# One constant matmul of 384 columns behind each of the 69 hops of a walk back

## The chip, the cores and the metric

The kernel runs on one core of a Trainium2 chip. The metric is the device time of one execution in microseconds (us); the figure of a kernel is the median of its runs.

## The reference, cut to what matters

Two gated layers over a hidden state of 8 batches of 56 tokens of 128 numbers, with a context of 8 x 1500 rows of 128 numbers. The first step aligns the 1500 context rows of a batch with its 56 tokens by dynamic time warping: a cost matrix, a path walked back from its last cell, and the context rows summed per token along the path.

```python
D = _pairwise_euclidean(small, large)
R = _dtw_cost(D)              # R[i,j] = D[i,j] + min(up, left, diagonal)
i_idx, j_idx, valid = _backtrack(R, T_small, T_large)
contrib = small[i_idx] * valid[:, None]
expanded = zeros((T_large, d)).at[j_idx].add(contrib)
...
x = x + tanh(g_xattn[0]) * _L0_xattn_ref(ctx_1024, layernorm(x))   # the alignment
x = x + tanh(g_ffn[0]) * _L0_ffn_ref(layernorm(x), ...)            # memory of 8192 rows, best row per head
x = x + tanh(g_xattn[1]) * _L1_xattn_ref(layernorm(x), ctx, ctx)   # attention, 16 heads, needs keys and values of ctx
x = x + tanh(g_ffn[1]) * _L1_ffn_ref(layernorm(x), ...)            # 8 experts
```

## The kernel before, in words

The program is written out by hand, one block per engine, with semaphores between them; there is no planner, so the order of the source is the order of each queue.

The alignment puts 16 lanes of a batch on 16 partitions (8 batches, 128 partitions), a lane holding C = 100 context rows. VectorE (DVE) scans the cost matrix in STEPS = 70 steps, step by step. TensorE (PE) meanwhile projects the keys of the attention layer (`keys_of`, `take_off`) and turns comparisons into jump codes (`jump_codes`, L1343 to L1347: three float16 matmuls with 404 or 400 columns, the first of `one16` by `steps16`, both constants). The codes go into banks 2 and 3; DVE reads each (`jump_targets`) and so gets, for every row, where the path leaves the lane.

Then the walk back: 69 hops, h = 0 to 68. Per hop DVE finds the entry for each lane (L1214, a comparison over 202 numbers with an accumulated sum, which reads the result of the last hop as its scalar from bank 2) and raises `s_hit`; PE spreads it over the lanes of the batch by one float16 matmul of one column with the constant weights `blk16` (L1403), and raises `s_hop`, for which the next L1214 waits. In between, PE works off the value projections (L1356, float32, 128 rows of context by the 128 columns of `Wv_sb`): there are 96 of them, 16 come before the walk and 80 in it. So 58 hops are followed by one value and 11 by two. A value shows as two records in the trace. ScalarE (ACT) copies groups of four out of their banks (L679). In the queue of PE the part around the change reads:

```python
pe.wait_ge(s_hit, h + 1)
nc.tensor.matmul(ps[2][:, t - 1:t], blk16[:, :], acc[:, t - 1:t], ...).then_inc(s_hop, 1)
...
for i in range(values, due):
    value(i)
```

After the walk DVE places the results (L1220, L1223), PE spreads them in two float32 matmuls of 284 columns (L1415, into banks 0 and 1), DVE copies them (L1229), and PE folds two weight matrices into bank 3 (L1421, eight float32 matmuls of 64 columns). ACT (L691) and DVE (L1238) then make 60 masks, 15 for each of four groups, and PE sums context rows under them (L1434), group by group; the masks of a third group wait until the sums of the first are done. Then come the layer norm (L1253, L1259), the memory layer with its gathers on GpSimd (POOL, L543), attention and the experts.

Bank 3 is read for the last time before the walk by the last `jump_targets` on DVE, which stands ahead of the first L1214 in DVE's queue; it is written next by the fold L1421.

Of the kernel before, what the change touches and what calls it, by code (L numbers as in the profile page):

```python
# [27 lines left out]
def build_gated_layers(nc, x_T, ctx_T, ctx_nat, g_xattn, g_ffn, weights, fold_w, w_tab, W1, W2, out):  # L28
# [5 lines left out]
    C = 100  # L34
# [18 lines left out]
    TB = 5  # L53
# [45 lines left out]
    with ExitStack() as ctx:  # L99
        def sb(name, shape, dt=F32):  # L100
            return ctx.enter_context(nc.sbuf_tensor(name, shape, dt))
# [5 lines left out]
        ps = [banks[:, i, :] for i in range(8)]  # L107
# [52 lines left out]
        steps16 = sb("steps16", [P, TB * SLOT], F16)  # L160
# [14 lines left out]
        def weight(n):  # L175
            nonlocal at
            at += n
            return wts[:, at - n:at]

        Wk_sb, cols = weight(D), weight(3)  # L180
# [14 lines left out]
        one16 = sb("one16", [P, P], F16)  # L195
# [229 lines left out]
        def _(sp):  # L425
# [23 lines left out]
            def load_key_parts(b):  # L449
                for c, (kx, _) in enumerate(PRODUCTS):  # L450
                    if b < 2 and c >= 2:
                        sp.wait_ge(s_kpl[b][c % 2], 16 * (c // 2))
                    sp.dma_start(KP[b % 3][c:NPR:len(PRODUCTS), :, :],
                                 key_parts[b, kx].rearrange("(m r) i -> r m i", r=2 * DH)
                                 ).then_inc(s_kpl[b % 3][c % 2], 16)
# [355 lines left out]
        def _(ve):  # L811
# [88 lines left out]
            def memory_layer():  # L900
# [42 lines left out]
                for c, (_, qx) in enumerate(PRODUCTS):  # L943
                    last = nc.vector.tensor_copy(picks[:, :, qx, c::len(PRODUCTS)], own)
# [305 lines left out]
        def _(pe):  # L1250
# [29 lines left out]
            def turn(u):  # L1280
# [6 lines left out]
                                               sd[:, u % D_RING, s * C:(s + 1) * C], ident[:, :])  # L1287
                last.then_inc(s_turn, 1)

            pe.wait_ge(s_mw, 1)  # L1290
            pe.wait_ge(s_x, 16)
            for i, (lo, hi) in enumerate(PAIR_COLS):
# [57 lines left out]
            def value(i):  # L1350
                n, k = i // 4, i % 4
                b, c = i // NCH, i % NCH
                if k == 0 and n >= 6:
                    pe.wait_ge(s_vc, n - 5)
                rows = min(P, NI - c * P)
                last = nc.tensor.matmul(ps[VALUE_BANKS[n % 6]][0:rows, k * D:(k + 1) * D],  # L1356
                                        ctxT[:, b * NI + c * P:b * NI + c * P + rows], Wv_sb, start=True, stop=True)
                if k == 3:
                    last.then_inc(s_vp, 1)
# [40 lines left out]
            for h in range(STEPS - 1):  # L1400
                t = STEPS - 1 - h
                pe.wait_ge(s_hit, h + 1)
                nc.tensor.matmul(ps[2][:, t - 1:t], blk16[:, :], acc[:, t - 1:t], start=True, stop=True  # L1403
                                 ).then_inc(s_hop, 1)
                if h == 0:
                    pe.wait_ge(s_kx[2], NKP)
                due = EARLY_VALUES + (h + 1) * (NB * NCH - EARLY_VALUES) // (STEPS - 1)
                for i in range(values, due):
                    value(i)
                values = due  # L1410
# [3 lines left out]
            for half in range(2):  # L1414
                last = nc.tensor.matmul(ps[half][0:C, 0:NB // 2 * ZW], ones[:, 0:C],  # L1415
                                        zt[:, half * NB // 2:(half + 1) * NB // 2, :].rearrange("p b j -> p (b j)"),
                                        start=True, stop=True)
# [147 lines left out]
            for b in range(NB):  # L1565
                pe.wait_ge(s_nmc, b + 1)
                for c in range(NCH):
# [5 lines left out]
                    for m in range(NH // 2):  # L1573
                        if m % 4 == 0 and len(units) > 1:
                            row_scores(*units.pop(0))
                        bank = ps[2 + 2 * (g % 2) + m // (NH // 4)]
# [135 lines left out]
```

## Time and profile before

| | before |
|---|---|
| median of 3 runs | 553.11 us (550.53, 553.89, 553.11) |
| the profiled execution | 552.93 us |
| its span, first to last instruction | 551.2 us |
| mean granted clock of TensorE over the span | 0.849 |
| PE busy | 425.8 us (77%), 3768 matmul records |
| DVE busy | 375.4 us (68%) |
| ACT busy | 262.9 us (48%) |
| POOL busy | 86.1 us (16%) |

All times in rows count from the first instruction of the profiled execution. A record of a matmul runs from its start to a modelled end, and matmuls are pipelined, so records overlap and a row merges those that touch. A granted clock of 1.00 is 2.4 GHz, 0.50 is 1.2 GHz. "Idle before" in brackets is the time that an engine stood still, with what released it.

### The profile page before, as it was taken

The page shows a single profiled execution, that of the slowest core. Times are in us where ns is not written, and L with a number is a line of the kernel's source. Part 1 is how long each engine was busy: PE and PEld are TensorE (multiplying, and loading weights), DVE is VectorE, ACT ScalarE, POOL GpSimd, SP SyncE. Part 2 cuts the span into 40 slices and gives each one's busy share as a digit, 9 for nine tenths or more (in the row PEclk, how much of TensorE's full clock was granted, in tenths as well). Part 3 has the DMA queues.
Part 4 walks back from the last instruction along what each step waited for, and adds up shares of the span by engine and source line. Part 5 has one row for each costly group of instructions (what it writes and reads, how often), then busy time and mean ns, then how long its engine had stood idle before and what let it go on. Part 6 is the DMA issues. An engine that isn't in the chain of part 4 may idle for free.

```text
span 551.2 us, 9665 instructions
## 1 busy us (share of the span) xinstructions
PE 425.8 (77%) x3768; PEld 253.9 (46%) x3768; DVE 375.4 (68%) x993; ACT 262.9 (48%) x449; POOL 86.1 (16%) x101
## 2 busy tenths in 40 slices
PE   3997887658999796300328789989999999779995
PEld 1443333326777594100113356656666666444442
DVE  7557999997555684876676668878889882361112
ACT  4365888665322491100101166656666667524442
POOL 2000000001000005687970000210210211000000
PEclk9999999998555687655558599999999999959999
DMA  8500564325412104953170002572573490000000
GB/s 288 202 1 1 172 202 156 107 84 153 135 57 68 44 3 111 220 149 88 35 168 0 0 1 39 133 167 56 119 168 83 90 298 11 3 0 0 0 1 17
DMA packets 28701, 50.03 MB, mean 91 GB/s; under 512 B 2448, under 2 KB 18384, under 8 KB 28656
## 3 DMA queue, kind: packets, MB, share of 16 engines
q1 hardware_dynamic: 26832, 45.74, 31.1%
q0 software_dynamic: 1536, 3.67, 2.5%
q8 instruction: 30, 0.49, 0.4%
q14 instruction: 15, 0.12, 0.1%
q10 hardware_dynamic: 288, 0.00, 0.0%
HBM read 39.96 MB, written 9.45 MB: 90 GB/s over the span
## 4 chain that ended last, share of the span: by engine, by line
PE 53%; DVE 30%; issue 7%; POOL 6%; ACT 2%; DMA 1%; DVEq 0%; POOLq 0%
PE banks L1356 9%; PE banks L1526 7%; PE banks L1550 7%; DVE mx L1005 6%; POOL arena L543 6%; PE banks L1578 5%; DVE arena L1185 5%; PE banks L1620 5%; PE banks L1628 4%; PE banks L1494 3%; PE banks L1271 2%; DVE work L1180 2%; PE banks L1434 2%; PE banks L1275 2%; DVE arena L1181 2%
## 5 line engine op out<-in xcount | busy, mean ns | idle before, releaser
L1005 DVE TENSOR_REDUCE mx<-banks 112x1 f32<-112x500 f32 x192 | 121.2, 675 | 25.4 <-PE banks L1526 25.4
L769 ACT ACTIVATE arena<-banks 128x896 f32<-128x896 f32 x96 | 87.9, 917 | 49.2 <-PE banks L1578 48.5
L1526 PE MATMUL banks<-ctxT,arena 128*112 128x500 bf16 x144 | 57.6, 411 | 7.4 <-issue 3.4
L1356 PE MATMUL banks<-wts,ctxT 128*128 128x128 f32 x192 | 57.9, 442 | 0.0
L1550 PE MATMUL banks<-arena 128*32 128x112 f32 (+1 forms) x1536 | 57.1, 265 | 1.0 <-ACT arena L769 0.8
L1214 DVE SCALAR_TENSOR_TENSOR work<-twice,banks,arena 128x202 f32<-128x202 f32 x68 | 29.5, 434 | 22.7 <-PE banks L1403 22.7
L1356 PEld LDWEIGHTS banks<-wts,ctxT 128*128 128x128 f32 x192 | 44.2, 295 | 1.0 <-ACT arena L679 0.3
L1550 PEld LDWEIGHTS banks<-arena 128*32 128x32 f32 (+1 forms) x1536 | 33.6, 109 | 21.1 <-issue 18.4
L1578 PEld LDWEIGHTS banks<-arena,ctxT 128*128 128x128 bf16 (+1 forms) x576 | 37.4, 104 | 10.5 <-issue 2.8
L1578 PE MATMUL banks<-arena,ctxT 128*128 128x112 bf16 (+1 forms) x576 | 40.9, 213 | 0.6 <-issue 0.6
L543 POOL DMA_INDIRECT arena<-in_w_tab,idx x32 | 33.9, 1060 | 12.6 <-issue 9.4
L1185 DVE TENSOR_TENSOR_SCAN arena<-work,arena 128x100 f32<-128x100 f32 x70 | 29.8, 426 | 7.4 <-ACT work L622 5.0
L1326 PE MATMUL banks<-arena,minusb 128*128 128x375 bf16 x64 | 19.9, 331 | 17.8 <-ACT arena L631 15.0
L637 ACT ACTIVATE arena<-banks,wts 128x375 bf16<-128x375 f32 x64 | 33.4, 581 | 0.5 <-PE banks L1326 0.5
L784 ACT ACTIVATE arena<-banks,wts 128x448 f32<-128x448 f32 x32 | 20.2, 633 | 27.2 <-PE banks L1620 27.2
L679 ACT ACTIVATE arena<-banks 128x512 f32<-128x512 f32 (+2 forms) x32 | 14.2, 493 | 38.1 <-PE banks L1356 35.7
L1620 PE MATMUL banks<-xnT,arena 128*128 128x448 f32 x64 | 32.2, 593 | 0.0
L1480 PE MATMUL banks<-ident,x_tok 112*128 112x112 f32 x4 | 1.2, 414 | 38.1 <-DVE x_tok L961 38.1
L1526 PEld LDWEIGHTS banks<-ctxT,arena 128*112 128x112 bf16 x144 | 18.7, 130 | 24.6 <-issue 11.9
L1628 PE MATMUL banks<-arena 128*128 128x448 f32 x64 | 29.6, 548 | 0.0
L1136 DVE SCALAR_TENSOR_TENSOR xc<-banks,wts,arena 128x448 f32<-128x448 f32 x7 | 4.8, 684 | 35.3 <-PE banks L1628 35.3
L576 POOL TENSOR_TENSOR work<-arena,mk 128x448 f32<-128x448 f32 x7 | 6.5, 932 | 133.1 <-ACT arena L746 133.1
(253 smaller groups left out, 741.3 us busy)
## 6 DMA issues: line engine op xcount, KB each, us to landing
ctxT<-key_parts SPq DMA_DIRECT2D x36, 375.0 KB, 6.5
key_parts<-arena SPq DMA_DIRECT2D x32, 281.2 KB, 2.8
ctxT<-in_ctx_T SPq DMA_DIRECT2D x12, 500.0 KB, 8.8
arena<-key_parts SPq DMA_DIRECT2D x12, 375.0 KB, 7.3
ctxT<-in_ctx_nat SPq DMA_DIRECT2D x5, 750.0 KB
arena<-in_ctx_nat SPq DMA_DIRECT2D x3, 750.0 KB
arena<-in_L_ffn_W SPq DMA_DIRECT2D x1, 2048.0 KB, 9.5
arena<-in_fold_w SPq DMA_DIRECT2D x1, 768.0 KB, 6.0
```

The source lines that it names most:

```text
L543: nc.gpsimd.indirect_dma_start(out=gath[:, t, h, :], out_offset=None, in_=w_tab[:, :], in_offset=bass.IndirectOffsetOnAxis(ap=idx[:, c:c + ...
L637: nc.scalar.activation(kq[m % STORES][:, x, :], ps[KBANKS[m % KRING]][:, 0:KPIECE], ACT.Identity, bias=cols[:, 1:2]).then_inc(s_kx[x], 1)
L769: nc.scalar.activation(Pt[0:rows, g % 2, :].rearrange("p (a n) -> p a n", a=2), banks[0:rows, 2 + 2 * (g % 2):4 + 2 * (g % 2), 0:HQ // 2], ...
L1005: nc.vector.tensor_reduce(mx3[:, b % 2, u // NPIECE, u % NPIECE:u % NPIECE + 1], ps[k % (6 if b == 0 else 2)][0:2 * NJ, 0:PIECE], AX_X, AL ...
L1185: nc.vector.tensor_tensor_scan(view(R, [[1, C]], (t + 1) * SLOT + 1), m, d, R[:, (t + 1) * SLOT:(t + 1) * SLOT + 1], ALU.min, ALU.add).the ...
L1214: nc.vector.scalar_tensor_tensor(out=hit_at.rearrange("p (c k) -> p c k", k=2), in0=twice[:, :].rearrange("p (c k) -> p c k", k=2), scalar ...
L1356: last = nc.tensor.matmul(ps[VALUE_BANKS[n % 6]][0:rows, k * D:(k + 1) * D], ctxT[:, b * NI + c * P:b * NI + c * P + rows], Wv_sb, start=T ...
L1526: nc.tensor.matmul(ps[k % ring][0:2 * NJ, 0:PIECE], QP[:, u // NPIECE, b, :], KP[b % 3][:, u // NPIECE, (u % NPIECE) * PIECE:(u % NPIECE + ...
L1550: last = nc.tensor.matmul(ps[6 + b % 2][q:q + 32, o:o + 2 * NJ], vals[0:rows, v0:v0 + 32], Pt[0:rows, g % 2, 2 * t * NJ:2 * (t + 1) * NJ], ...
L1578: last = nc.tensor.matmul(bank[0:rows, o:o + 2 * NJ], KP[b % 3][:, m, c * P:c * P + rows], QP[:, m, b, :], start=True, stop=True)
L1620: nc.tensor.matmul(ps[5 + i % 2][:, 0:TOK], W1s[:, e, c * P:(c + 1) * P], xnT[:, :], start=True, stop=True).then_inc(s_h, 1)
L1628: nc.tensor.matmul(ps[7 if e % 2 else 0][:, 0:TOK], W2s[:, i, :], hT[:, i % 4, :], start=(c == 0), stop=(c == FC - 1)).then_inc(s_yu, 1)
```

## The change

Behind each hop's matmul PE issues one more: `one16` (128 x 128, float16) as weights, the first 384 columns of `steps16` (float16) as the moving operand, into bank 3, with no semaphore wait and none raised. Nobody reads what it writes. It stands ahead of the values of that hop; there are 69 of them.

```diff
+            def keep_busy(bank, n, cols=TB * C):
+
+                for _ in range(n):
+                    nc.tensor.matmul(bank[:, 0:cols], one16[:, :], steps16[:, 0:cols], start=True, stop=True,
+                                     skip_group_check=True)
+
...
                 pe.wait_ge(s_hit, h + 1)
                 nc.tensor.matmul(ps[2][:, t - 1:t], blk16[:, :], acc[:, t - 1:t], start=True, stop=True
                                  ).then_inc(s_hop, 1)
+                keep_busy(ps[3], 1, 384)
                 if h == 0:
                     pe.wait_ge(s_kx[2], NKP)
```

## Rows read from the trace of the kernel before

**Rows 1.** The page: tenths of PE busy, and granted clock, in 40 slices.
```profile
PE   3997887658999796300328789989999999779995
...
PEclk9999999998555687655558599999999999959999
```

**Rows 2.** Stretches: busy us of PE, PEld, DVE, ACT, POOL; clock; DMA share; GB/s.
```profile
100.00:120.00 20.00, 12.87 (x55) 5.97 (x53) 19.26 (x76) 13.28 (x27) 0.00 (x0) 1.00 0.29 96
...
130.90:132.50 1.60, 1.14 (x8) 0.77 (x9) 0.89 (x4) 1.57 (x3) 0.00 (x0) 1.00 0.97 257
132.50:183.80 51.30, 51.30 (x218) 39.04 (x217) 29.33 (x132) 14.48 (x32) 1.59 (x3) 0.50 0.36 105
183.80:187.20 3.40, 3.40 (x13) 2.48 (x12) 1.31 (x4) 0.65 (x2) 0.00 (x0) 0.51 0.00 0
187.20:192.70 5.50, 1.72 (x16) 1.58 (x15) 4.97 (x17) 4.66 (x16) 0.00 (x0) 0.80 0.00 1
192.70:198.50 5.80, 5.70 (x64) 5.74 (x66) 4.24 (x15) 5.80 (x22) 0.00 (x0) 0.60 0.01 3
198.50:211.00 12.50, 11.63 (x186) 10.16 (x182) 8.12 (x31) 9.03 (x33) 0.00 (x0) 1.00 0.01 2
```

**Rows 3.** The chain that ended last, in the walk: start, us, what.
```profile
133.27 0.64 PE banks L1356 x2
```

**Rows 4.** Groups by line, 130.9 to 183.9 us: busy, mean ns, idle before.
```profile
L1214 DVE SCALAR_TENSOR_TENSOR work<-twice,banks,arena 128x202 f32<-128x202 f32 x68 | 29.5, 434 | 22.7 <-PE banks L1403 22.7
...
L1403 PE MATMUL banks<-acc,blk 128*128 128x1 f16 x69 | 13.1, 190 | 1.1 <-DVE work L1214 1.1
```

**Rows 5.** Instructions in order of time, two hops at the half clock.
```profile
150.16 0.10 PEld L1403 LDWEIGHTS banks<-acc,blk 128*128 128x128 f16 x1 [0.20 <-DVE work L1214]
150.16 0.19 PE L1403 MATMUL banks<-acc,blk 128*128 128x1 f16 x1
...
150.21 1.20 PE L1356 MATMUL banks<-wts,ctxT 128*128 128x128 f32 x4
...
150.38 0.43 DVE L1214 SCALAR_TENSOR_TENSOR work<-twice,banks,arena 128x202 f32<-128x202 f32 x1 [0.28 <-PE banks L1403]
150.74 0.09 DVE L1214 DVE_READ_ACCUMULATOR work<-twice,banks,arena 128x1 f16 x1
...
151.20 0.21 PE L1403 MATMUL banks<-acc,blk 128*128 128x1 f16 x1
...
151.28 0.78 PE L1356 MATMUL banks<-wts,ctxT 128*128 128x128 f32 x2
...
151.95 0.10 PEld L1403 LDWEIGHTS banks<-acc,blk 128*128 128x128 f16 x1 [0.20 <-DVE work L1214]
```

**Rows 6.** Matmuls in order of time, at the full clock.
```profile
127.74 0.34 PE L1343 MATMUL banks<-steps,one 128*128 128x404 f16 x1 [0.57 <-DVE work L1163]
127.92 0.33 PE L1345 MATMUL banks<-work,one 128*128 128x400 f16 x1
...
130.94 0.18 PE L1403 MATMUL banks<-acc,blk 128*128 128x1 f16 x1 [0.72 <-DVE work L1214]
130.98 0.47 PE L1356 MATMUL banks<-wts,ctxT 128*128 128x128 f32 x2
131.66 0.18 PE L1403 MATMUL banks<-acc,blk 128*128 128x1 f16 x1 [0.21 <-DVE work L1214]
```

**Rows 7.** Instructions in order of time, from the last hop to the masks.
```profile
183.84 0.19 PE L1403 MATMUL banks<-acc,blk 128*128 128x1 f16 x1
...
184.93 2.22 PE L1415 MATMUL banks<-work,ones 128*100 128x284 f32 x4
...
187.19 0.81 DVE L1229 COPY work<-banks 100x284 f32<-100x284 f32 x2 [1.78 <-PE banks L1415]
```

**Rows 8.** Instructions in order of time, where the sums begin.
```profile
192.80 5.78 PE L1434 MATMUL banks<-arena 100*56 100x128 f32 x61 [3.88 <-issue]
...
198.53 7.55 DVE L1238 SCALAR_TENSOR_TENSOR arena<-work,rowc 100x112 f32<-100x112 f32 x30 [1.18 <-PE banks L1434]
```

## The prediction

> **What bounds the kernel now.** I read the page's slices first [rows 1]: PE is busy in nine tenths of the slices of the walk, and yet its clock stands at 0.5 there. The stretches say it more closely [rows 2]: 1.00 in the keys stage and in the first 1.6 us of the walk, then 0.50 in the whole of 132.5 to 183.8 us, where the records of PE cover 51.30 us of 51.30. That cover is not load: the records of matmuls reach beyond the array's own work.
>
> The chain of waits puts most of a hop on the value matmuls [rows 3], which would make PE the bound. The instructions in order of time correct this [rows 5]. In the usual hop PE's weight load for the hop has stood idle for 0.20 us and is released by DVE (row of 151.95): the loop is DVE's 0.43 us, the 0.09 us of the accumulator read and the hop's own 0.19 us with the hand-overs between. The groups agree: 68 comparisons take 29.5 us and wait another 22.7 us for the hop [rows 4]. So the walk is a loop of latencies between DVE and PE, and values ride along in its gaps.
>
> Two things in this loop depend on PE's clock. First, a hop with two values. At the half clock one value's records end 0.78 us after their start and two values' 1.20 us [rows 5]: 0.42 to 0.43 us per value. After two of them the next hop comes 151.20 - 150.16 = 1.04 us after the last, where a usual gap is 0.725 us, and it is not released by DVE but stands behind the values. Second, a little in each gap: at the full clock it is 131.66 - 130.94 = 0.72 [rows 6], more closely 0.717 us in the first three gaps, against 0.725 to 0.727 at the half clock. The gap behind a late hop is itself 0.03 us longer.
>
> **The change, part by part.** It removes and moves nothing. It adds 69 matmuls of 384 float16 columns with one weight load each, no wait and no semaphore. DVE, ACT, POOL and SP issue the same instructions in the same order.
>
> *(a) Cost of one.* Two matmuls of 404 and 400 columns start 127.92 - 127.74 = 0.18 us apart at the full clock [rows 6], so 384 columns take about 0.17 us there, and 0.33 us at half. Its weight load has no row of its own kind; I bound it between nothing (hidden, as the value matmuls at 0.43 us apart leave no sign of theirs) and 0.10 us, the hop's own weight load [rows 5]. I take 0.03.
>
> *(b) Does it lie on the loop?* It stands behind the hop, so it can only delay the next one. After the hop, the array's work apart from values is 1.04 - 2 x 0.427 = 0.19 us. At the full clock, one value: 0.19 + 0.21 + 0.17 + 0.03 = 0.60 us, under 0.717: hidden behind DVE's comparison. Two values: 0.81 us, 0.09 over. But the 0.19 was read at the half clock and part of it (the 0.10 us weight load) should shrink; the other reading, by the end of the records (0.05 + 0.47 + 0.21 + 0.17 less the 0.2 us by which a hop starts ahead of the end of the values), gives 0.70, no delay. I take 0.04 us for each of ten such gaps (the eleventh double hop is the last): **+0.4 us**, bounds 0 and +1.1.
>
> *(c) What it does to the clock.* This is the point of decision. In the first 1.6 us of the walk the engine was still at 1.00 from the keys stage and fell after two hops with values alone; the array then had 0.25 us of value work in 0.717 (80 values over 69 hops, 0.213 us each). With the filler it has 0.25 + 0.17 = 0.42 us, 58% of the hop. The keys stage holds 1.00 with records that cover 12.87 of 20 us [rows 2], which overstate the array's part just as they do here, so the filled walk is at least as loaded as a stage that never fell. And should the clock fall nevertheless before the walk, the filled hop at half clock is nearly all work (0.495 + 0.33 of about 0.94 us), like 183.8 to 187.2, where values, the spread and the fold followed one another and the clock rose at the end [rows 2]. I forecast 1.00 through the walk.
>
> By the Trainium skill (TensorE: Matmul & The Clock Gate, Why this matters for your kernels) drops come from long pauses between bursts of matmuls, with no word on short ones. The walk's pauses are 0.2 us by these rows and it sat at 0.50, so the rule as worded doesn't hold here; by it the filler would change nothing in the clock, and only its cost would remain, which is rival A.
>
> *(d) The walk.* It runs from 130.94 [rows 6] to 183.84 [rows 7], 52.90 us in 68 gaps. At 0.717 each it is 48.76: -4.1 us, with (b) **-3.7 us**. Split: the ten late gaps give 10 x (1.04 - 0.725 + 0.03) = 3.5, the rest is the 0.01 us in each gap. If the short gap was due to something else, only 3.5 - 0.4 = 3.1.
>
> *(e) Behind the walk.* L1415 starts 1.09 us after the last hop, its records take 2.22 us and DVE's copy comes at 187.19 [rows 7]. It is 2 x 284 float32 columns, by the value (128 columns, 0.427 us) 1.89 us of array at half clock, 0.95 at full: **-0.95 us**, if the clock lasts one or two us beyond the walk. Bounds: 0 and -1.0. The fold behind it is hidden by ACT's and DVE's masks.
>
> *(f) The sums.* PE then stands idle for 3.88 us, the first sums run mostly at the half clock (0.60 in 192.7 to 198.5 [rows 2]) and the masks of the third group wait 1.18 us for them [rows 8]. The idle stretch remains, so the clock will fall again; how much of the first sums it catches is chance: between -1.2 and +1.1 us (all at half). I take 0. The same chance moves later stages that hover between the levels by perhaps 1 us to either side; the three runs of before are 3.4 us apart.
>
> *(g) Afterwards* the memory layer, attention and experts start earlier by what was won; they hang on the chain, and the gathers' requests go out when the indices are there, so nothing gives it back. Loads of context rows are released by values and come earlier.
>
> Sum: -3.7 - 0.95 = -4.65, so 552.93 - 4.65 = 548.3 us for the profiled execution. That lies 0.2 below the median, within its spread; I keep **548.3 us**.
>
> **Rivals.**
> A, the clock falls all the same and stays at 0.50: the filler's constants don't count for it, or not enough. Then PE becomes the bound. A hop with one value takes 0.19 + 0.43 + 0.33 = 0.95 us instead of 0.725, one with two 1.37 instead of 1.04: 58 x 0.22 + 10 x 0.33 = +16 us, **569 us**. It decides as soon as the array's work at the granted clock exceeds 0.72 us per hop. For it: 51 us at half in spite of short pauses. Against it: hops that are 0.83/0.95 work, like the stretch after which the clock rose. 5%.
>
> B, the clock swings between the levels in the walk. If the half clock has a third of the walk, 23 hops cost 0.22 us each, +5 us, against two thirds of the win (-3): with (e) half lost, about **+1.5, 554.5 us**. Against it: the filled hop is well above the loaded stretches that held. 9%.
>
> C, the clock holds, but two-value hops stay late and the chance of (f) goes wrong: -3.7 - 0.7 + 0.95 lost from (e) + 1.1: about -2.4, **550.6 us**; its opposite, (f) and a later stage won, about -7.0, 546. These are the ends of the first case (86%) rather than cases of their own.
>
> D, the filler brings nothing since the late hops are hidden elsewhere: the walk has no parallel work that ends after it, as DVE goes straight from the last hop to L1220. Under 1%.
>
> **How the numbers follow.** The main case has 86%: 548.3, itself between 545.6 and 551. B and A have 9 and 5. The range for 8 in 10 leaves out A, most of B and the low tail: **545.4 to 552.6**. About 1% (5.5 us) is what a measurement of this kernel can tell from no change; below 547.6 lies some 38% of the main case: faster 0.33. Slower than 558.6 only A and a bad B: 0.06. Within 1%: 0.61.
>
> **What would show it.** (c): the granted clock is 1.00 from 131 to the end of the walk. (d): 68 gaps of 0.717 us, a walk of 48.8 to 49.9 us, comparisons that wait about 19 us rather than 22.7. (b): gaps after two values at 0.72 to 0.83. (e): the copy L1229 some 2.3 us after the last hop rather than 3.35. (f): the wait of the third group's masks between 0 and 2.3 us. A clock at 0.50 with gaps near 0.95 would make the prediction wrong by its first step.

## The result and the profile after

The changed kernel takes **547.08 us** (median of 4 runs, 545.44 to 548.34) against 553.50 for the kernel before; the ratio is 0.9891, 95% interval 0.9844 to 0.9938, so 3 to 9 us are won. Ten further runs, timed beside 25 of the kernel before, give 546.72 against 551.86, ratio 0.9898 (0.9857 to 0.9938). The forecast was 548.3 us, in a range of 545.4 to 552.6. The profiled execution took 546.93 us, with a span of 545.2.

The granted clock in slices on the page of the changed kernel, to be held against [rows 1]:

```profile
PEclk9998999978999887655558599999999999959999
```

The slices of the walk, 5 before, are 9 now. Elsewhere there are a few new dips (slices 4, 9, 10): the clock fell for one or two short stretches ahead of the walk in this execution.

Stretches of the changed kernel, in the columns of [rows 2]: the end of the keys stage, the walk, spread and fold, idle PE, first sums, the remaining sums.

```profile
120.00:133.40 13.40, 9.58 (x54) 6.68 (x54) 13.05 (x43) 7.21 (x16) 0.00 (x0) 0.87 0.25 83
133.40:182.40 49.00, 41.02 (x292) 28.85 (x292) 30.18 (x136) 15.90 (x34) 1.59 (x3) 1.00 0.41 118
182.40:185.80 3.40, 3.07 (x22) 2.59 (x23) 2.12 (x5) 0.84 (x3) 0.00 (x0) 1.00 0.00 0
185.80:190.20 4.40, 0.66 (x6) 0.52 (x5) 4.09 (x15) 4.40 (x16) 0.00 (x0) 0.72 0.01 2
190.20:196.00 5.80, 5.62 (x66) 5.65 (x68) 4.38 (x17) 5.80 (x22) 0.00 (x0) 0.62 0.00 0
196.00:208.50 12.50, 11.61 (x185) 10.12 (x180) 8.07 (x31) 9.14 (x33) 0.00 (x0) 1.00 0.01 3
```

PE has 69 more matmuls in the walk and is busy for less of it: 41.02 of 49.00 us, where it was 51.30 of 51.30 [rows 2]. Behind the walk the picture is that of before: the clock falls in the idle stretch and the first sums start at the half clock.

Groups by line, 133.3 to 182.5 us, and a hop with two values in order of time (L1409 is the hop, L1293 the filler, L1362 the values):

```profile
L1214 DVE SCALAR_TENSOR_TENSOR work<-twice,banks,arena 128x202 f32<-128x202 f32 x68 | 29.5, 434 | 18.9 <-PE banks L1409 18.9
L1362 PE MATMUL banks<-wts,ctxT 128*128 128x128 f32 (+1 forms) x156 | 28.3, 273 | 0.3 <-ACT arena L679 0.3
...
L1293 PE MATMUL banks<-steps,one 128*128 128x384 f16 x69 | 22.3, 323 | 0.0
```

```profile
137.70 0.18 PE L1409 MATMUL banks<-acc,blk 128*128 128x1 f16 x1
...
137.74 0.32 PE L1293 MATMUL banks<-steps,one 128*128 128x384 f16 x1
...
137.91 0.60 PE L1362 MATMUL banks<-wts,ctxT 128*128 128x128 f32 x4
137.92 0.43 DVE L1214 SCALAR_TENSOR_TENSOR work<-twice,banks,arena 128x202 f32<-128x202 f32 x1 [0.27 <-PE banks L1409]
...
138.42 0.18 PE L1409 MATMUL banks<-acc,blk 128*128 128x1 f16 x1
...
139.12 0.49 PE L1362 MATMUL banks<-wts,ctxT 128*128 128x128 f32 x2 [0.34 <-ACT arena L679]
...
139.45 0.17 PE L1409 MATMUL banks<-acc,blk 128*128 128x1 f16 x1
```

DVE waits 18.9 us for the hop where it waited 22.7 [rows 4]; its own work is the same 29.5. The hop behind two values and a filler comes 138.42 - 137.70 = 0.72 us after the last: hidden. The next is late by 0.31 us for a cause of its own: the value waits for ACT (row of 139.12), whose first copy stood behind POOL's fill of the value tiles. That is the only gap of 68 that isn't 0.711 to 0.719.

From one profiled execution to the other, by milestones (us from the first instruction):

| | before | after | difference of the stretch |
|---|---|---|---|
| first hop | 130.94 | 133.40 | +2.46 |
| last hop | 183.84 | 182.44 | -3.86 |
| copy L1229 | 187.19 | 184.77 | -1.02 |
| first row maximum | 296.61 | 293.99 | -0.20 |
| end of the last row maximum | 456.88 | 450.88 | -3.38 |
| store of the output | 548.20 | 542.22 | +0.02 |

The walk and the spread give 4.9 us. The other two large entries, +2.46 ahead of the first added matmul and -3.38 in attention, are put down to chance: the first lies ahead of anything that was changed, and both stretches vary by as much between the profiles of the experiments.

### The profile page after: what moved, and what is told of

It is laid out like the page before. It is cut to its first block, busy times and chain, and to the rows that moved or that the text cites. A ratio compares the mean times of both kernels' runs of the same rounds, so it can differ in the third digit from the quotient of the medians.

```text
span 545.2 us, 9803 instructions
## 1 busy us (share of the span) xinstructions
PE 418.6 (77%) x3837; PEld 245.2 (45%) x3837; DVE 375.3 (69%) x993; ACT 263.0 (48%) x449; POOL 86.2 (16%) x101
## 4 chain that ended last, share of the span: by engine, by line
PE 49%; DVE 33%; issue 8%; POOL 6%; ACT 2%; DMA 2%; DVEq 0%; POOLq 0%
PE banks L1557 7%; PE banks L1533 7%; DVE mx L1005 7%; POOL arena L543 6%; PE banks L1585 5%; PE banks L1627 5%; DVE work L1214 4%; DVE arena L1185 4%; PE banks L1635 4%; PE banks L1501 3%; PE banks L1271 2%; PE banks L1409 2%; PE banks L1275 2%; PE banks L1441 2%; DVE work L1180 2%
## 5 line engine op out<-in xcount | busy, mean ns | idle before, releaser
L1214 DVE SCALAR_TENSOR_TENSOR work<-twice,banks,arena 128x202 f32<-128x202 f32 x68 | 29.5, 434 | 18.9 <-PE banks L1409 18.9
L1362 PE MATMUL banks<-wts,ctxT 128*128 128x128 f32 x192 | 34.1, 279 | 0.3 <-ACT arena L679 0.3
L1332 PE MATMUL banks<-arena,minusb 128*128 128x375 bf16 x64 | 21.0, 349 | 14.9 <-ACT arena L631 12.4
L1362 PEld LDWEIGHTS banks<-wts,ctxT 128*128 128x128 f32 x192 | 31.4, 192 | 1.0 <-ACT arena L679 0.6
L1635 PE MATMUL banks<-arena 128*128 128x448 f32 x64 | 29.5, 546 | 0.0
L1325 PE MATMUL banks<-ctxT,wts 128*128 128x375 f32 x64 | 28.6, 534 | 0.8
```

The source lines that it names most:

```text
L1214: nc.vector.scalar_tensor_tensor(out=hit_at.rearrange("p (c k) -> p c k", k=2), in0=twice[:, :].rearrange("p (c k) -> p c k", k=2), scalar ...
L1635: nc.tensor.matmul(ps[7 if e % 2 else 0][:, 0:TOK], W2s[:, i, :], hT[:, i % 4, :], start=(c == 0), stop=(c == FC - 1)).then_inc(s_yu, 1)
```

## The experiments

Each is a variant of the changed kernel unless it says otherwise, and was timed beside the kernel before on the same chip. The walk is the time from the first to the last hop in the profiled execution, the clock in the walk is that execution's, and the last column has the mean granted clock over the whole span in every run that was timed. That column tells more than the one profile does: it is at most 0.853 in every run of the kernel before, and at least 0.885 in every run with 384 or 192 columns behind all hops.

| | ratio to before (95%) | median | clock in the walk | walk | last hop to copy | span clock, all runs |
|---|---|---|---|---|---|---|
| before (first profile) | 1 | 551.86 to 553.5 | 1.00, then 0.50 | 52.90 | 3.35 | 0.837 to 0.853 |
| 384 columns, again | 0.9898 (0.9857 to 0.9938) | 546.72 | 1.00 | 48.89 | 2.32 | 0.887 to 0.899 |
| 192 columns | 0.9862 (0.9788 to 0.9936) | 544.65 | 1.00 | 48.73 | 2.32 | 0.896 to 0.898 |
| 96 columns | 0.9949 (0.9920 to 0.9978) | 549.76 | 1.00, then 0.50 | 53.15 | 2.52 | 0.848 to 0.888 |
| 1 column | 0.9971 (0.9931 to 1.0010) | 550.19 | 1.00, then 0.50 | 53.10 | 3.34 | 0.841 to 0.851 |
| zeros | 0.9873 (0.9831 to 0.9916) | 545.15 | 1.00 | 48.99 | 2.32 | 0.895 to 0.901 |
| lighter second value, no filler | 0.9967 (0.9932 to 1.0002) | 550.49 | 1.00, then 0.50 | 50.66 | 3.03 | 0.845 to 0.855 |
| two fillers | 0.9938 (0.9902 to 0.9974) | 549.80 | 1.00 | 49.65 | 2.32 | 0.889 to 0.898 |
| filler from hop 20 | 0.9923 (0.9899 to 0.9947) | 549.13 | 1.00, 0.50, 1.00 | 50.19 | 2.32 | 0.875 to 0.886 |
| bridge to the sums | 0.9897 (0.9861 to 0.9933) | 547.25 | 1.00 | 48.88 | 2.32 | 0.894 to 0.907 |
| more fillers | 0.9837 (0.9783 to 0.9891) | 543.93 | 1.00 | 48.74 | 2.32 | 0.912 to 0.923 |

**The changed kernel again.**

> The changed kernel once more, for the ratio and for what varies between executions. Theory (the filler holds PE's clock in the walk and the spread behind it): granted clock 1.00 in the walk, 68 gaps of 0.717 us, walk 48.8 to 49.1 us, copy of the spread 2.3 us after the last hop; time 5 us below before. The further 3.4 us between the first and the last row maximum are, by this theory, waits for key parts that land late by chance: that stretch may take anything from 157 to 161 us here. Rival (the shift in time aligns the loads better): 157 us again, and the time again 6 us below.

Walk and copy came as expected. From the first to the last row maximum (starts) it took 154.7 us, against 159.6 before and 156.2 in the first profile after: below the range that I had set, so the verdict comes from all profiles together. In the twelve of this study that stretch took 154.5 to 164.7 us, with the longest value in a kernel whose walk was fast (filler from hop 20), and 155.4 in the one with 1 column, whose walk is that of before; so a faster walk does not go with a short attention stage. In the kernel before, one such wait is this one (the chain, then the DMA queues from 369 to 372 us):

```profile
369.20 0.93 ACT arena L769
370.13 2.02 issue
372.15 0.42 PE banks L1526
```

```profile
q1 hardware_dynamic: 218, 0.59, 91.4%
q8 instruction: 1, 0.02, 2.5%
```

What PE could wait for, ACT's exponential, ended at 370.13; for 2.02 us more PE waited for nothing that the profile shows. One packet of the instruction queue (q8) is moved from 369.4 to 370.6 us, while key parts (q1) fill the DMA engines. So my "key parts that land late" was the wrong reading: no semaphore of that load is waited for here. That PE stood without instructions, whose loading shares the engines with the key parts, is a guess that was not tested, and the rows speak for it only weakly: the packet had landed 1.6 us before PE went on, and of the 18 packets of that queue in this stage, the others have no wait of PE of over 1 us beside them. The cause stays open. The first hop, too, came at 130.9 to 131.3 us in seven of the twelve profiles and at 133.3 to 134.1 in five, in kernels of every sort, though none differs before it but for one memset in the kernel with zeros.

**One column.**

```diff
-                keep_busy(ps[3], 1, 384)
+                keep_busy(ps[3], 1, 1)
```

> The filler has 1 column instead of 384: same instructions and weight loads, hardly any streaming. Theory (load on the array keeps the clock): clock 0.50 from the third hop on, late hops of 1.04 to 1.1 us behind two values, walk 52.9 us, time as before (within 1 us). Rival (it is the number of instructions or weight loads that the clock looks at): clock 1.00, walk 49 us, 5 us faster than before.

```profile
131.30:134.90 3.60, 2.66 (x20) 1.72 (x20) 2.22 (x10) 2.57 (x4) 0.32 (x1) 1.00 0.89 244
134.90:184.40 49.50, 49.47 (x272) 39.42 (x272) 27.98 (x126) 13.57 (x30) 1.27 (x3) 0.50 0.33 98
```

The stretches of this kernel's walk: the clock falls as in the kernel before, here some hops later, and the late gaps are 1.07 us, 0.03 more than before. The mean clock of all ten runs (0.841 to 0.851) is that of the kernel before. The instructions and weight loads alone do nothing for the clock; the streaming does. The median is 1.7 us below before, more than the 1 us that I allowed, but the interval of the ratio includes 1.

**192 columns, and 96.**

```diff
-                keep_busy(ps[3], 1, 384)
+                keep_busy(ps[3], 1, 192)
```

> The filler has 192 columns. Theory: the array then works 0.25 + 0.08 = 0.33 of 0.717 us; still like the keys stage, so clock 1.00, walk 48.8 us, same time as with 384. Rival (384 is needed): clock 0.50 or swinging; at 0.50 a gap of 0.19 + 0.43 + 0.16 = 0.78 us, walk about 57 us, 4 us slower than before.

> The filler has 96 columns instead of 384 or 192: the array streams for 0.25 + 0.04 of 0.717 us. Theory (what holds the clock is the load, with less of it somewhere between 1 column, which did not hold it, and 192, which did): either outcome fits; if it holds, walk 48.8 us and 6 us below before; if it falls, gaps of 0.727 and late ones near 1.08, walk 53 us, time 1 to 2 us below before. A swing between both would show as stretches of either gap.

The second run has `keep_busy(ps[3], 1, 96)` in the same place. Stretches of the walk, 192 columns first, then 96:

```profile
130.90:179.60 48.70, 37.99 (x292) 25.35 (x292) 30.18 (x136) 15.98 (x34) 1.59 (x3) 1.00 0.39 118
```

```profile
133.50:137.00 3.50, 2.66 (x20) 1.72 (x20) 2.16 (x10) 2.56 (x4) 0.29 (x1) 1.00 0.91 260
137.00:186.70 49.70, 49.58 (x273) 39.40 (x274) 28.04 (x128) 13.56 (x30) 1.30 (x3) 0.50 0.32 97
```

192 held the clock throughout and 96 did not, in the one profile of each. The mean clock of the other runs shows that the profile with 96 columns is not the whole story: its twelve runs spread from 0.848, as in this profile, to 0.888, as with 384 columns, and nine of them lie above every run of the kernel before. So with 96 columns the clock most likely held for part of the walk in most executions, and for nearly all of it in two (0.887 and 0.888); no trace of those runs shows where. That also fits the time: the ratio of 0.9949 is clear of 1 (some 2.8 us), though the profiled walk is no shorter than before. With 192 columns all four runs lie at 0.896 to 0.898. The records show why "busy" misleads here: the held walk is covered for 38 of 49 us, the fallen one for all of it. With 192 columns no gap was late. Its time is at least as good as with 384; the intervals overlap.

**Zeros.**

```diff
+                nc.tensor.matmul(bank[:, 0:cols], zero16[:, 0:P], zero16[:, 0:cols], start=True, stop=True, ...
```

> The filler of 384 columns multiplies zeros by zeros. Theory (the clock follows how long the array streams, not the values): clock 1.00 in the walk, 68 gaps of 0.717, same time as with the constants. Rival (zeros don't count): clock 0.50, gaps of 0.95, walk 68 us, time 568 us.

```profile
130.90:179.90 49.00, 41.01 (x292) 28.85 (x292) 30.18 (x136) 16.04 (x34) 1.59 (x3) 1.00 0.41 117
```

Not shown in the diff: the tile `zero16` and the one memset on DVE that fills it. The clock stays at 1.00 on zeros, and the mean clock of all four runs is that of the constants. What is multiplied doesn't matter here.

**Late hops taken away at the half clock.** The kernel before, without filler:

```diff
                 for i in range(values, due):
-                    value(i)
+                    if i > values and i % 4 != 3:
...
+                        nc.tensor.matmul(ps[VALUE_BANKS[i // 4 % 6]][:, i % 4 * D:(i % 4 + 1) * D], one16[:, :],
+                                         steps16[:, 0:D], start=True, stop=True)
+                    else:
+                        value(i)
```

> The kernel before, without filler; behind hops with two values the second is one float16 matmul of 128 columns instead of a float32 value in 8 of 10 such gaps (those 8 values are wrong). It takes away most late hops while the clock stays low. Theory (3.5 of the walk's 3.9 us are the late hops): clock 0.50, gaps behind two values 0.73 instead of 1.04 in 8 places, walk 52.9 - 8 x 0.34 = 50.2 us, spread still at the half clock (copy 3.3 us after the last hop), time 2.5 to 3 us below before. Rival (the gap itself depends on the clock by much more than 0.01 us): walk above 52 us, time as before.

```profile
143.48 0.19 PE L1403 MATMUL banks<-acc,blk 128*128 128x1 f16 x1
143.53 0.78 PE L1356 MATMUL banks<-wts,ctxT 128*128 128x128 f32 x2
144.10 0.31 PE L1412 MATMUL banks<-steps,one 128*128 128x128 f16 x1
144.21 0.21 PE L1403 MATMUL banks<-acc,blk 128*128 128x1 f16 x1
```

PE's matmuls in order of time: behind the lightened pair the hop comes 144.21 - 143.48 = 0.73 us after the last. The walk shrank to 50.66 us at a clock of 0.52. It still has three late gaps: two of 1.04 behind pairs of values left whole, and 1.06 once, where ACT's first copy comes. Without the eight lightened ones the walk lost 2.24 us of the 3.86, which confirms that late hops are most of what the low clock costs. The forecast of 2.5 to 3 us in the kernel's time is not confirmed: the ratio is 0.9967, and its interval allows anything from nothing to 3.8 us.

**Two fillers.**

```diff
-                keep_busy(ps[3], 1, 384)
+                keep_busy(ps[3], 2, 384)
```

> Two fillers of 384 columns behind each hop. It prices what the first one was near to costing. In the changed kernel two values and one filler (0.43 + 0.16 us) fit into 0.717 us, so the array's other work in a hop is at most 0.13 us at the full clock. Theory (PE delays a hop only where values and fillers exceed what DVE hides): after one value 0.13 + 0.21 + 0.32 = 0.66 us, hidden, gaps 0.717; after two values 0.88, so ten gaps 0.10 to 0.20 us longer; walk 49.8 to 50.9 us, clock 1.00, time 1 to 2 us above the kernel with one filler. Rival (each filler costs a fixed part of every hop): gaps of 0.75 or more throughout, walk above 51 us.

```profile
137.83 0.18 PE L1409 MATMUL banks<-acc,blk 128*128 128x1 f16 x1
...
137.87 0.49 PE L1293 MATMUL banks<-steps,one 128*128 128x384 f16 x2
...
138.19 0.60 PE L1362 MATMUL banks<-wts,ctxT 128*128 128x128 f32 x4
...
138.64 0.16 PE L1409 MATMUL banks<-acc,blk 128*128 128x1 f16 x1
```

In order of time: two fillers and two values make the next hop late by 0.09 us (0.80 to 0.81 in ten gaps), after one value it stays at 0.717. The walk is 49.65 us, 0.15 under the forecast. By the ratios the kernel is some 2 us above the one with one filler, of which the walk accounts for 0.8; its profile also had one of the long attention stages (160.4 us). The intervals of the two ratios overlap, so more than the 0.8 isn't shown.

**Filler from hop 20 on.**

```diff
+                if h >= 20:
+                    keep_busy(ps[3], 1, 384)
```

> The 384-column filler only from hop 20 on, so that the clock falls first. Theory (a filled hop at the half clock is nearly all work, and that raises the clock again): 0.50 from about the third hop to some hops behind the 20th, there gaps of 0.93 to 0.95 us until it rises to 1.00, then 0.717 to the end; walk 50.5 to 52.5 us, copy of the spread 2.3 us after the last hop. Rival (filler can hold the clock, not raise it): 0.50 to the end, 48 gaps of 0.95, walk above 62 us, time 10 us slower than before.

Four stretches of this walk, and matmuls of PE at hops 20 and 21, the first with a filler, at the half clock:

```profile
130.90:135.30 4.40, 3.13 (x20) 2.00 (x20) 2.66 (x12) 2.52 (x4) 1.12 (x1) 1.00 0.89 251
135.30:145.50 10.20, 10.13 (x44) 7.91 (x44) 5.78 (x26) 4.99 (x12) 0.47 (x3) 0.50 0.45 150
145.50:149.00 3.50, 3.50 (x20) 3.01 (x19) 1.77 (x8) 0.60 (x1) 0.00 (x0) 0.50 0.63 187
149.00:181.10 32.10, 26.99 (x194) 19.01 (x193) 19.96 (x90) 7.98 (x17) 0.00 (x0) 1.00 0.26 76
```

```profile
146.48 0.19 PE L1409 MATMUL banks<-acc,blk 128*128 128x1 f16 x1
146.53 0.48 PE L1293 MATMUL banks<-steps,one 128*128 128x384 f16 x1
146.80 0.63 PE L1362 MATMUL banks<-wts,ctxT 128*128 128x128 f32 x2
147.23 0.21 PE L1409 MATMUL banks<-acc,blk 128*128 128x1 f16 x1
```

The filler raises a fallen clock too, and did so at 149.0 us, within the fourth filled hop. But such a hop at the half clock takes 0.75 to 0.78 us (147.23 - 146.48 = 0.75), not the 0.93 to 0.95 that I had added up. The clock fell only in the seventh hop, not about the third. The walk is 50.19 us, 0.3 under my range for that reason. The late fall of its clock cost the walk 1.3 us against a filler from the start.

**Bridge to the sums.**

```diff
             pe.wait_ge(s_vc, NCH // 4 * NB)
+            keep_busy(ps[2], 20, 384)
```

> The changed kernel with 20 more fillers of 384 columns between the fold and the first sums, where PE stands idle for 3.9 us. Theory: they fill 3.2 us of it at the full clock, the first sums run at 1.00 instead of 0.50, the masks of the third group no longer wait 1.2 us for them; 1.0 to 1.3 us less from the last hop to the hidden state, time 1.2 us below the changed kernel. Rival (the fillers run into the first sums and delay them): the same stretch as long or longer.

The idle stretch, and the first sums (start of 60 records), in stretches:

```profile
185.80:190.00 4.20, 3.60 (x24) 2.05 (x22) 4.16 (x15) 4.20 (x16) 0.00 (x0) 1.00 0.01 2
190.00:193.50 3.50, 3.48 (x60) 3.27 (x60) 3.11 (x12) 3.50 (x14) 0.00 (x0) 1.00 0.02 5
```

The mechanism came as forecast and the gain did not. The first sums take 3.5 us instead of 5.6, and the masks of the third group no longer wait. Yet from the last hop to the hidden state (L906) it takes 23.25 us, against 23.44 and 23.63 in the two profiles of the changed kernel, and the time is the same too (ratio 0.9897 against 0.9898). The chain shows where it went; first the changed kernel, then this one:

```profile
190.38 5.53 PE banks L1441 x60
195.91 0.02 issue
195.94 3.34 DVE arena L1238 x14
199.27 0.11 issue
199.38 4.13 DVE arena L1238 x16
```

```profile
185.31 4.29 ACT work L691 x15
...
194.64 4.14 DVE arena L1238 x15
198.78 0.04 issue
198.82 4.19 DVE arena L1238 x15
```

Behind the wait of 1.0 us the first 14 masks took 3.34 us (0.24 each), because ACT had worked ahead in the meantime; without the wait each takes 0.28, at ACT's pace (4.29 us for 15). The removed wait comes back as slower masks, 0.8 of 1.0 us.

The other profiles bear this out and give it a limit. Among those where the copy comes 2.32 us after the last hop, the masks of the third group waited 0.65 us with two fillers, 1.20 in the changed kernel's second profile, 1.51 with zeros and 1.85 with 192 columns, and the hidden state came 23.25, 23.63, 23.93 and 24.27 us after the last hop. So the first 0.7 to 0.8 us of the wait cost nothing, and what lay beyond counted in full.

**More fillers**, with 192 columns in the walk (the comments say where each stands and are not in the kernel):

```diff
-                keep_busy(ps[3], 1, 384)
+                keep_busy(ps[3], 1, 192)
...
+            keep_busy(ps[2], 20, 384)      # ahead of the first sums
...
+            keep_busy(ps[2], 10, 384)      # ahead of tokens(0)
...
+            keep_busy(ps[5], 18, 384)      # ahead of the query rows
...
                 row_scores(0, u)
+                keep_busy(ps[7], 1, 384)
...
+            keep_busy(ps[2], 6, 384)       # ahead of the router's logits
```

> The 192-column filler in the walk, and fillers of 384 columns at four more places where PE waits at the half clock: 20 between the fold and the first sums, 10 before the first memory similarities, 18 before the query rows L1494 of attention (7 us of idle PE), one behind each of the 24 row-score matmuls of the first batch, and 6 before the router's logits. Theory (PE work on the chain in these places ran at 0.50): the query rows' 6.3 us shrink by 2 us, the first similarities by 0.9 us, the second half of the query rows by 1 to 2 us, the first hidden tiles by 0.5 to 1 us: 4 to 5 us below the changed kernel, about 541.5 us. Rival (each stage has another engine right behind PE, as ACT stood behind the first sums in the last experiment): 1 us or less below the changed kernel.

The chain of this kernel at the first similarities (L1459), the first half of the query rows, and the second (both L1503):

```profile
211.09 1.13 PE banks L1459 x2
...
282.10 5.84 PE banks L1503 x21
...
303.87 7.56 PE banks L1503 x24
```

The first similarities lost the 0.9 us (2.03 before, now 1.13). The query rows lost 0.5 of the hoped-for 2 (6.30 before; 6.14 in the changed kernel), and the second half, which lies behind the first row maximum, still fell into a stretch at 0.50. From the last hop to the first row maximum it takes 109.96 us against 111.5 in both profiles of the changed kernel: 1.5 us, where the terms forecast for this part, 2 and 0.9, come to 2.9. That stretch alone took 111.3 to 112.8 us in the seven other profiles with the clock at 1.00 at the end of the walk, so some of the 1.5 can be chance. Behind the last row maximum, where 0.5 to 1 us were hoped for, nothing was won: 94.3 us to the last instruction, as in the changed kernel and the one before. The kernel has the lowest median of all, 543.93 against 552.63 for before. It beats the kernel before clearly; against the one with 192 columns alone (544.65) and the changed one (546.72) the intervals overlap.

## Why the prediction was right, step by step

- **(c), the clock**: held. 1.00 in all of the walk [rows 2 for before: 0.50]. With 1 column it fell, with zeros it held, and a fallen clock rose again under the filler. So it is streaming that counts. My reason "as loaded as the keys stage" was too loose: with 96 columns the clock fell in the profile and held for part of the walk in other runs, though records covered the held walk less than the fallen one. The step gave the right sign with a margin that I could not have read from busy times. Rival B, a clock that swings, is what 96 columns seem to bring; with 384 it did not come.
- **(d), the walk**: -3.7 forecast, -3.86 measured (52.90 to 49.05), -4.0 in the second profile. That the first comes so close is luck in part: the 0.4 us charged for (b) did not occur, and 0.31 us was lost in one gap for another cause. With 192 columns, where no gap was late, the walk lost 4.17, near the 4.1 forecast before (b). Its split held too: with most of the late hops taken away at the half clock, 2.24 us went, and ordinary gaps are 0.717 at one level and 0.727 at the other, as the first three gaps had shown.
- **(b), the filler's own cost**: 0.4 forecast, none measured. The bound of zero was the true one: two values and one filler fit under DVE's comparison, and even two fillers cost only 0.09 us per such gap. The rest of the hop's work at the full clock is about 0.06 us (0.81 - 0.43 - 0.32), not the 0.19 read at the half clock. What came instead is one late gap of 1.03 us, where ACT's first copy waits for POOL (that gap is 0.85 to 1.03 in four profiles, and not late in the two with 192 columns).
- **(e), the spread**: -0.95 forecast, -1.02 measured.
- **(f), the sums**: taken at 0, measured -0.2. Its bound of -1.2 was wrong in kind: without any wait the hidden state comes 23.25 us after the last hop, and with the wait of 1.2 us 23.63, so that wait is worth 0.4, as ACT sets the pace of the masks when PE no longer does. The other side was real: with 192 columns the wait was 1.85 us and cost 0.6 more.
- **(g)**: nothing is given back. The store comes 91.3 us after the end of the last row maximum in both. The size of chance was too small, though: I allowed about 1 us for stages hovering between levels, and attention varies by 10 us between profiles, the start by 2 to 3.
- **Rival A** was too dear by my arithmetic. At the half clock a filled hop with one value takes 0.75 to 0.78 us, so its price is about 0.04 us for each of 58 hops and, by an estimate, 0.15 to 0.3 for each of ten (two values and a filler at the half clock take at least 2 x 0.427 + 0.33 = 1.18 us against 1.04; no such hop was run): 4 to 5 us and not 16. The sum 0.19 + 0.43 + 0.33 counted the 0.19 in full, and nearly all of it disappears when a filler stands between the hop and the value. Why is only argued: the value's weight load then has a matmul to hide behind.
- **Rival C** has a slip in its sum: late hops would take 0.7 us off the win, not add to it, and (e) was not in the -3.7. By its own terms it is -3.7 + 0.7 + 1.1 = -1.9, 551.0 us. It did not occur, and the range hardly changes by it.
- **Sum**: -4.65 forecast; walk, spread and sums give -5.1 in the first pair of profiles, and the medians differ by 6.4 us in the first timing and by 5.1 in the second. What the first has beyond 5.1 is not explained by any of the terms, and lies within its interval.

## What to carry to other kernels

A stretch in which PE's records cover everything can still be one in which its clock has fallen: look at the granted clock beside the busy share, and at what releases the instruction that matters. In a loop of latencies, cheap matmuls that nobody reads can buy back the clock, if they fit into the time another engine needs anyway; try a few sizes, for both too few columns (1 gained nothing, 96 only part) and too many (late hops) lose. One profile is one execution: with 96 columns it showed the low clock, and only the mean clock of the other runs told that this was not always so. Before a wait is removed, ask whether the engine behind it used the wait to work ahead.

## What was not expected of the hardware

- Records of PE covered 49.6 of 49.7 us at the half clock with a filler of 96 columns, and 38.0 of 48.7 us at the full clock with 192: the cover of the records says little of the load.
- The clock fell one to three times ahead of the walk in each of the eleven later profiles (slices 4, 9 and 10 of the page above), and not at all in the one of before, in code that is the same in all kernels but for the one memset.
- The stretch from first to last row maximum, the same code in all kernels but the one with more fillers, took between 154.5 and 164.7 us in twelve profiles, with waits of up to 2.5 us in it that the profile puts down to no engine.
